# One scan instruction for a whole state, PE's work in whole states, and a diagonal product in every fourth state

## The reference

```python
xs, z = split(h @ in_w);  xs = silu(xs);  proj = xs @ xproj_w     # xs: (L, 512)
dt = softplus(proj[..., :512] + dt_bias)                          # per token and channel
Bm, Cm = proj[..., 512:576], proj[..., 576:]                      # 64 states each
def step(hst, ins):                                               # over the 256 tokens
    hst = hst * exp(dt_t[:, :, None] * A) + (dt_t * x_t)[:, :, None] * B_t[:, None, :]
    y_t = einsum('bds,bs->bd', hst, C_t)
y = ys + xs * Dskip;  return y * silu(z) @ out_w
```

## Time and profile before

| | |
|---|---|
| median of 3 runs (lowest, highest) | 3402.99 us (3399.81, 3408.39) |
| profiled execution, its own time | 3408.53 us |
| its span, first to last instruction | 3406.7 us |
| mean granted TensorE clock | 0.947 |
| PE, ACT, POOL, DVE busy | 3024.2, 2989.0, 2945.7, 2909.5 us |

### The profile page before, as it was taken

One profiled execution on the slowest core, in us unless ns is written; L12 is line 12 of the kernel. 1 busy time (PEld: TensorE's weight loads), 2 busy tenths in 40 slices (PEclk: granted clock), 3 DMA queues, 4 the chain that ended last, 5 costly groups with the idle time before them and its releaser, 6 DMA issues.

```text
span 3406.7 us, 69419 instructions
## 1 busy us (share of the span) xinstructions
PE 3024.2 (89%) x21944; PEld 2683.9 (79%) x21944; DVE 2909.5 (85%) x3331; ACT 2989.0 (88%) x6469; POOL 2945.7 (86%) x1552
## 2 busy tenths in 40 slices
PE   8778898999988999899988999899998899998776
PEld 6568787888878888788877888788887888887765
DVE  3269998899888998889988999889988899899885
ACT  1189999899989999899999999899998999999994
POOL 0069998999888998889988998889988899899995
PEclk6689999999989999899999999899998999999998
DMA  4011111111111111111111111112111111111210
GB/s 174 0 42 43 48 45 47 42 51 48 43 48 47 47 47 42 49 45 48 45 47 43 49 48 43 48 41 52 48 43 46 48 47 46 42 45 45 54 47 26
DMA packets 163033, 162.50 MB, mean 48 GB/s; under 512 B 17610, under 2 KB 156874, under 8 KB 162644
## 3 DMA queue, kind: packets, MB, share of 16 engines
q1 hardware_dynamic: 162644, 157.69, 17.2%
HBM read 154.44 MB, written 3.18 MB: 46 GB/s over the span
## 4 chain that ended last, share of the span: by engine, by line
PE 45%; POOL 16%; ACT 15%; issue 13%; DVE 9%; DMA 1%; DVEq 1%; POOLq 0%; ACTq 0%; SPq 0%
POOL hst L408 12%; PE ps L1225 12%; PE ps L1241 11%; ACT dA L567 7%; PE ps L993 6%; ACT uBT L553 4%; DVE hst L892 4%; PE ps L1002 4%; POOL uBT L417 4%; PE ps L1065 3%; PE ps L1040 2%; PE ps L1114 1%; PE ps L1049 1%; PE ps L1233 1%; PE ps L1150 1%
## 5 line engine op out<-in xcount | busy, mean ns | idle before, releaser
L408 POOL TENSOR_TENSOR hst<-hst,C_sb 128x1024 f32<-128x1024 f32 x1024 | 2441.0, 2409 | 232.8 <-DVE hst L892 226.6
L892 DVE TENSOR_TENSOR_SCAN hst<-dA,ps 128x512 f32<-128x512 f32 x2048 | 2384.0, 1205 | 177.6 <-PE ps L1241 160.1
L567 ACT ACTIVATE dA<-dt,A 128x255 f32<-128x255 f32 x4096 | 1758.5, 504 | 2.8 <-DVE hst L892 2.7
L1225 PE MATMUL ps<-ident,uBT 128*128 128x128 f32 x8192 | 1288.2, 281 | 134.0 <-DVE hst L892 103.0
L1241 PE MATMUL ps<-ident,hst 128*128 128x128 f32 x8192 | 1267.9, 278 | 104.5 <-POOL hst L408 103.7
L1225 PEld LDWEIGHTS ps<-ident,uBT 128*128 128x128 f32 x8192 | 994.2, 145 | 299.0 <-DVE hst L892 152.5
L553 ACT ACTIVATE uBT<-uT,BT 128x512 f32<-128x512 f32 x1536 | 1052.2, 720 | 130.9 <-PE ps L1225 120.0
L1241 PEld LDWEIGHTS ps<-ident,hst 128*128 128x128 f32 x8192 | 979.6, 144 | 139.8 <-POOL hst L408 139.7
L417 POOL TENSOR_TENSOR uBT<-uT,BT 128x512 f32<-128x512 f32 x512 | 559.3, 1092 | 185.3 <-DVE uT L829 185.3
L476 ACT ACTIVATE probs<-ps,nmax 128x128 f32<-128x128 f32 (+1 forms) x256 | 93.9, 423 | 101.6 <-DVE nmax L764 100.7
L993 PE MATMUL ps<-xsT,w_xp 128*128 128x256 f32 x512 | 130.6, 380 | 0.0
(11 more groups left out here) (142 smaller groups left out, 2110.7 us busy)
## 6 DMA issues: line engine op xcount, KB each, us to landing
C_sb<-c_dram SPq DMA_DIRECT2D x1024, 128.0 KB, 2.9
gate_l<-gate_rows_dram SPq DMA_DIRECT2D x16, 256.0 KB, 3.7
x_att<-in_x_dram SPq DMA_DIRECT2D x8, 256.0 KB, 3.0
w<-in_L_cond_W_dram SPq DMA_DIRECT2D x2, 1024.0 KB
out_dram<-x_glu SPq DMA_DIRECT2D x8, 256.0 KB, 3.2
wg<-in_L_cond_mlp_w_dram SPq DMA_DIRECT2D x3, 512.0 KB, 11.4
w_xp<-_L_cond_fwd_xproj_w_dram SPq DMA_DIRECT2D x1, 1280.0 KB, 12.4
w_xp<-_L_cond_bwd_xproj_w_dram SPq DMA_DIRECT2D x1, 1280.0 KB, 15.0
```

Of the source, the lines that this page charges most:

```text
L408: pool.tensor_tensor(h, h, C_sb[:, n % FED:n % FED + 1, :].to_broadcast([P, KI, NB]), ALU.mult).then_inc(hC_ready.sem, 1)
L567: done = act.activation(dA[:, n % NT, c, lo:hi], dt[:, d, c, lo:hi], ACT.Exp, scale=A[:, d, c, n:n + 1])
L892: dve.tensor_tensor_scan(pair(hst[:, n % NR]), pair(dA[:, n % NT]), ps[:, BANK_U + (2 * n + e) % (2 * NU), :][:, way], 0.0, ALU.mult, ALU. ...
L1225: last = pe.transpose(ps[:, BANK_U + (2 * n + e) % (2 * NU), o:o + P], uBT[:, n % NF, j, c * P:(c + 1) * P], ident[:, :])
```

## The change

Four things change.

1. DVE runs one scan instruction of 128x1024 for a state, in the slot e = 1. It waits for whole states: uB_ready, y_mm and scan_done have one event a state.
2. PE works in whole states: sum_state (8 transposes) in slot e = 0, force (8) in slot e = 1. Within a state, sum_state now comes ahead of force.
3. `gate_y` is one state earlier on DVE (ahead of scan 2, before it was between the halves of scan 3).
4. In every fourth state (n % 4 == 3) u is not multiplied by B on ACT and POOL. POOL writes a diagonal, the identity times B, for both halves of tokens (128x2x128 in place of 128x512), and PE computes force as the product of u with this diagonal (8 float32 products in place of 8 transposes). ACT's forcing of this state is gone.

```diff
@@ -43,6 +43,7 @@
     BEHIND = 3
+    by_diagonal = lambda n: n % 4 == 3
     FED = 4
...
@@ -277,8 +278,8 @@
         uT_mm, uT_ready = flow("uT_mm"), flow("uT_ready")
-        uBT_ready, uBT_pooled, uB_ready, dA_ready = flow("uBT_ready"), flow("uBT_pooled", NS // 2), flow("uB_ready", 2), flow("dA_ready", 2)
-        scan_done, hC_ready, y_mm = flow("scan_done", 2, 2 * NT), flow("hC_ready", 1, FED), flow("y_mm", 2, 2 * NR)
+        uBT_ready, uBT_pooled, uB_ready, dA_ready = flow("uBT_ready", NS - NS // 4), flow("uBT_pooled", NS // 2), flow("uB_ready"), flow("dA_ready", 2)
+        scan_done, hC_ready, y_mm = flow("scan_done", 1, NT), flow("hC_ready", 1, FED), flow("y_mm", 1, NR)
         block = ctx.enter_context(nc.Block())
...
@@ -403,7 +404,7 @@
                 pool.wait_ge(C_in[n % FED], (p * (NS // FED) + n // FED + 1) * 16)
-                pool.wait_ge(scan_done.sem, scan_done.at(p * NS + n, 2))
+                pool.wait_ge(scan_done.sem, scan_done.at(p * NS + n, 1))
                 h = hst[:, n % NR]
...
@@ -413,7 +414,11 @@
                 if r_known(p, n) >= NF:
-                    pool.wait_ge(uB_ready.sem, uB_ready.at(p * NS + n, 2 - 2 * NF))
+                    pool.wait_ge(uB_ready.sem, uB_ready.at(p * NS + n, 1 - NF))
+                if by_diagonal(n):
+                    pool.tensor_tensor(uBT[:, n % NF, :, 0:P], ident[:, :].unsqueeze(1).to_broadcast([P, TT, P]),
+                                       BT[:, d, :, n:n + 1].to_broadcast([P, TT, P]), ALU.mult).then_inc(uBT_pooled.sem, 1)
+                    return
                 pool.tensor_tensor(uBT[:, n % NF, 1, :], uT[:, d, DI:2 * DI], BT[:, d, 1, n:n + 1].to_broadcast([P, DI]), ALU.mult).then_inc(uBT_pooled.sem, 1)
...
@@ -543,12 +548,14 @@
             def forcing(p, d, n):
+                if by_diagonal(n):
+                    return
                 r = p * NS + n
...
                 if r_known(p, n) >= NF:
-                    act.wait_ge(uB_ready.sem, uB_ready.at(r, 2 - 2 * NF))
+                    act.wait_ge(uB_ready.sem, uB_ready.at(r, 1 - NF))
                 for j in range(TT - n % 2):
...
@@ -559,8 +566,8 @@
                     act.wait_ge(dt_ready.sem, dt_ready.at(p, 1))
-                if r_known(p, n) >= NT:
-                    act.wait_ge(scan_done.sem, scan_done.at(p * NS + n, (2 if n < NT else e + 1) - 2 * NT))
+                if e == 0 and r_known(p, n) >= NT:
+                    act.wait_ge(scan_done.sem, scan_done.at(p * NS + n, 1 - NT))
                 if n < NT and e == 0:
...
@@ -882,15 +889,18 @@
                 def state(n, e):
+                    if e == 0:
+                        return
                     r = p * NS + n
-                    if n == BEHIND and e == 1 and not very_first:
+                    if n == BEHIND - 1 and not very_first:
                         gate_y(p - 1, 1 - d)
-                    dve.wait_ge(y_mm.sem, y_mm.at(r, e + 1 - 2 * NR))
-                    dve.wait_ge(dA_ready.sem, dA_ready.at(r, e + 1))
-                    dve.wait_ge(uB_ready.sem, uB_ready.at(r, e + 1))
-                    pair = lambda t: t[:, 2 * e:2 * e + 2, :].rearrange("p k n -> p (k n)")[:, way]
-                    dve.tensor_tensor_scan(pair(hst[:, n % NR]), pair(dA[:, n % NT]),
-                                           ps[:, BANK_U + (2 * n + e) % (2 * NU), :][:, way], 0.0, ALU.mult, ALU.add).then_inc(scan_done.sem, 1)
+                    dve.wait_ge(y_mm.sem, y_mm.at(r, 1 - NR))
+                    dve.wait_ge(dA_ready.sem, dA_ready.at(r, 2))
+                    dve.wait_ge(uB_ready.sem, uB_ready.at(r, 1))
+                    bank = BANK_U + 2 * n % (2 * NU)
+                    line = lambda t: t.rearrange("p k n -> p (k n)")[:, way]
+                    dve.tensor_tensor_scan(line(hst[:, n % NR]), line(dA[:, n % NT]), line(ps[:, bank:bank + 2, :]),
+                                           0.0, ALU.mult, ALU.add).then_inc(scan_done.sem, 1)
                 return state
...
@@ -1210,19 +1220,23 @@
                 yield from glu(b)
-            def force(p, n, e):
+            def force(p, d, n):
                 r = p * NS + n
-                if e == 0:
-                    pe.wait_ge(uBT_ready.sem, uBT_ready.at(r, 1))
-                    if n % 2 == 1:
-                        pe.wait_ge(uBT_pooled.sem, uBT_pooled.at(p, n // 2 + 1))
+                if not by_diagonal(n):
+                    pe.wait_ge(uBT_ready.sem, uBT_ready.at(p, n + 1 - n // 4))
+                if n % 2 == 1:
+                    pe.wait_ge(uBT_pooled.sem, uBT_pooled.at(p, n // 2 + 1))
                 if r_known(p, n) >= NU:
-                    pe.wait_ge(scan_done.sem, scan_done.at(r, e + 1 - 2 * NU))
-                for c in range(2 * e, 2 * e + 2):
+                    pe.wait_ge(scan_done.sem, scan_done.at(r, 1 - NU))
+                for c in range(KI):
                     for j in range(TT):
                         o = c % 2 * NB + j * P
-                        last = pe.transpose(ps[:, BANK_U + (2 * n + e) % (2 * NU), o:o + P], uBT[:, n % NF, j, c * P:(c + 1) * P], ident[:, :])
+                        to = ps[:, BANK_U + (2 * n + c // 2) % (2 * NU), o:o + P]
+                        if by_diagonal(n):
+                            last = pe.matmul(to, uT[:, d, j * DI + c * P:j * DI + (c + 1) * P], uBT[:, n % NF, j, 0:P], start=True, stop=True)
+                        else:
+                            last = pe.transpose(to, uBT[:, n % NF, j, c * P:(c + 1) * P], ident[:, :])
                 last.then_inc(uB_ready.sem, 1)
...
@@ -1233,10 +1247,9 @@
                                   start=(c == 0), stop=False, skip_group_check=True)
-            def sum_state(r, n, e):
-                if e == 0:
-                    pe.wait_ge(hC_ready.sem, hC_ready.at(r, 1))
-                for c in range(2 * e, 2 * e + 2):
+            def sum_state(r, n):
+                pe.wait_ge(hC_ready.sem, hC_ready.at(r, 1))
+                for c in range(KI):
                     for j in range(TT):
...
@@ -1245,16 +1258,18 @@
                 def state(n, e):
-                    if n + 1 < NS:
-                        force(p, n + 1, e)
-                    elif not very_last:
-                        force(p + 1, 0, e)
-                    if n == BEHIND and e == 0:
+                    if e == 1:
+                        if n + 1 < NS:
+                            force(p, d, n + 1)
+                        elif not very_last:
+                            force(p + 1, 1 - d, 0)
+                        return
+                    if n == BEHIND:
                         start_y(p, d)
                     if n >= BEHIND:
-                        sum_state(p * NS + n - BEHIND, n - BEHIND, e)
+                        sum_state(p * NS + n - BEHIND, n - BEHIND)
                     elif not very_first:
-                        sum_state(p * NS + n - BEHIND, NS + n - BEHIND, e)
+                        sum_state(p * NS + n - BEHIND, NS + n - BEHIND)
                 return state
```

8 lines of the change are left out of this document (3 added, 5 removed).

## The result

The changed kernel took 3514.26 us (median of 4, 3510.59 to 3517.97), the kernel before 3403.38 us (4 runs beside it). The ratio is 1.0319, 95% interval 1.0303 to 1.0335: 111 us slower. The forecast was 21 us slower, so the sign held and the size did not.

What follows compares the result with a forecast made beforehand. PE was taken to bound some stages, ACT, POOL or DVE others; +4.4 us a pair over 6.5 pairs (+28.6) and -8 in the last pass made +21 us, 3424 us, 0.6% slower, range 3365 to 3475.

Steps and rivals of the forecast that it cites:

- order, whole states, gate_y: Start of a pass: start_y no longer waits for the earlier gate_y, -2.8 us a pair; whole states cost 0.
- products: Every fourth state on PE: 0.905 us more each, +9.1 in PE-full stretches, +0.9 at state 3, +2.0 in heads, a pair.
- relief of ACT and POOL: Every fourth state: less ACT forcing, -3.8 us a pair; POOL's smaller diagonal, -1.0 a pair and -8 in the last pass.
- The step that failed: PE between two scans: force fits by 1.1 us, by 0.2 in every fourth state, so whole states cost 0.
- The 13.2 charged products a pair: Products counted as paid on PE, out of 32 a pair: 10.0 in PE-full stretches, 1 at state 3, 2.2 in heads.
- The second half of the heads: In 1612 to 1662, 4.3 products cost between 0 and 3.9 us a pair; taken as +2.0.
- The last pass: POOL is full and products hide, so 16 smaller diagonals at 0.5 us save 8 us, counted whole, once.
- Passes 0 and 14: Half of the stages each, with losses and gains of 1 to 2 us that were let cancel.
- A (hidden products): PE-full stretches really paced by ACT and DVE, so products are paid half at most: 3385, or 3346 us; chance 0.30.
- B (DVE starves behind the products): In 1527 to 1594 and 1612 to 1662 every fourth scan starts up to 0.9 us late: 3470 us; chance 0.15.
- C (all paid): All 32 products of a pair are paid on PE: +21.4 us a pair, 3534 us; chance 0.02.
- D: Products bring PE's higher clock back sooner, saving up to half of 9.8 us a pair: 3392 us; chance 0.03.

Runs made afterwards that it cites:

- run 1: The changed kernel without diagonals (joined scan, PE in whole states, early gate_y) against the kernel before: 3427.44 us, ratio 1.0061.
- run 3: Diagonals, but 8 transposes of u for the products (B left out there): the changed kernel so cut took 3379.96 us, the same in the old order 3383.55 us.
- runs 2 to 4: Against the kernel before: diagonals alone, 3460.36 us; relief without products, 3379.96 (new order) and 3383.55 us (old); products with the identity, without relief, 3494.40 us.
- Run 6: The changed kernel with 4 products and 4 transposes of u in every fourth state (B left out of half of it): 3453.68 us, ratio 1.0140.
- run 10: The kernel before with diagonals only in passes 0, 14 (but for its state 3) and 15: 3383.43 us, ratio 0.9932.

## Why the prediction was right in sign and wrong in size

The forecast's own terms over the run beside what the experiments measured (us; each difference of two runs is good to some 8; "run 1" is experiment 1, and so on):

| term | forecast | measured |
|---|---|---|
| order, whole states, gate_y | -2.8 x 6.5 = -18 | +23 (run 1) |
| products | (9.1 + 0.9 + 2.0) x 6.5 = +78 | +77 in the old order, +134 in the new (run 3) |
| relief of ACT and POOL | (-3.8 - 1.0) x 6.5 - 8 = -39 | -21 in the old order (-34 beside the products), -47 in the new |
| sum | +21 | 23 + 134 - 47 = +110 |

**The step that failed** is the one on the order: "Waits for whole states leave less play [...] I take 0 and keep the loss as a rival". It was wrong twice. By itself the order costs 23 us, and 41 with the 18 us that I had credited to gate_y: the wait for gate_y fell from 21.0 to 7.7 us in run 1, but PE's wait for scans grew from 103.0 to 154.0, and its whole idle time by 32. And it raised the products' price from 77 to 134 us. Nearly all of that rise is PE's busy time (52 us), with the clock at its lower level for 134 us less in the old order and for only 21 less in the new; why the order takes the clock's gain away stays open, and the forecast had no term for it. The two errors are 41 + 56 = 97 of the miss of 89; relief was 8 better than forecast. In the old order the relief gave less, 21 us: it shortened passes 0, 14 and 15 by some 6 to 7 us each, but a pair in between by 0.2 where 4.8 were forecast. There the lower level took 36.1 us a pair in place of 27.3, and the 2.5 us lost in states 92 to 100 cancel what the other states had gained.

The argument for 0 was that force fits between two scans when these follow each other evenly. It said nothing of the states in which DVE is late with a scan because a chain step stands ahead of it, and there PE's wait is paid in full. It also leaned on DVE's waits for PE where PE is full. The largest piece that the order cost, 2.2 us in states 16 to 24, lies outside these stretches; the next, 1.2 us in 72 to 80, lies inside the heads, where PE, POOL and DVE were all full.

**The products.** Their duration was right (1.78 us). The 13.2 charged products a pair make 86 in the run, and 77 / 0.905 = 85 of 256 would be paid in the old order, in the new 134 / 0.905 = 148. That 86 and 85 meet is luck in part: the 77 us are 159 us more of busy time less 81 of idle time, and the clock, which the count leaves out, had given back up to 67. From start_y to the pass's first product for dt, the stretch that was 38.7 us (1400.81 to 1439.55) is now 41.65 (1446.34 to 1487.99), with three products in it: +2.9, forecast 2.7. The second half of the heads was priced too low. States 72 to 92, which cover the 50 us from 1612 and some more, went from 57.8 to 61.3 us with the diagonals alone, +3.5 where +2.0 was taken and 3.9 was my upper bound; with the order they take 64.0, +6.2. The chain of the kernel after in that stage (start, us, what) shows why:

```profile
1686.21 0.92 PE ps L1254 x8
1687.13 1.79 PE ps L1237 x16
1688.91 0.44 PE ps L1059 x4
1689.35 0.11 PE ps L1071 x2
1689.46 1.06 PE ps L1075 x4
1690.52 1.02 PE ps L1254 x8
...
1700.23 1.79 PE ps L1237 x16
```

There is nothing but PE between the two products, 13.1 us apart: PE did set the pace, and its pipelined ends did not hide idle time.

**Right.** The last pass: -8 forecast, 181.0 to 173.6 us measured (172.9 with diagonals alone). Passes 0 and 14, which I let cancel, were faster by 4.0 and 4.8 us with diagonals alone, a gain that I missed. The diagonal on POOL has a pitch of 0.573 us, near the 0.5 that I took. The joined scan saves nothing: its mean duration fell from 2 x 1205 to 2278 ns, but its pitch is 2 x 1.115 before and 2.20 after, as the DVE timeline of the kernel after shows:

```profile
1704.35 2.28 DVE L902 TENSOR_TENSOR_SCAN hst<-dA,ps 128x1024 f32<-128x1024 f32 x1
1706.55 0.14 DVE L756 RECIPROCAL rsum<-ps 128x2 f32<-128x2 f32 x1
```

**The rivals.** A (hidden products) fell at runs 2 to 4: the relief is real, but the products cost 77 us or more on either order. B (DVE starves behind the products) is right in part: DVE's idle time before its scans rose from 177.6 to 216.7 us, 39 us, where my mark was 40. But 23 of these 39 are there in run 1 without any product (200.5), and with the diagonals alone nothing rose (172.8). In its first stretch, where POOL was full (states 52 to 72), nothing was lost; in its second, the heads, PE itself was the bound. C (all paid) is 20 us from the result, by accident: 148 of 256 were paid, and the order gave the rest. D had the time wrong and the mechanism right: the diagonals alone cut the lower level from 27.3 to 17.0 us a pair and raised the mean granted clock from 0.947 to 0.962. That is up to 5 us a pair, which D forecast, and it lies inside the products' price: without it they would have cost more. The changed kernel has less of it (20.4 us a pair, 0.957). D counted 9.8 us a pair at the lower level, from two stretches; the trace before has 27.3. And the row against D, 7.86 of 11 us busy at full clock, shows that transposes can run at a full clock, not that they hold it as well as products do. The Trainium skill's factor of four for transposes ("TensorE: Matmul & The Clock Gate", Terms) would have put the time at 3570 us, which is nearer to the result than my forecast, and yet isn't its reason: the same eight products still take 1.78 us beside 0.88.

**Open.** The 31 us have no run of their own. By PE's busy and idle time the larger part goes with the clock and the smaller with idle time that is filled less well; why the products bring back less of the clock in the new order is not known. By states, 15 of the 31 lie at the hand-overs; the other 16 have no place yet. Run 6 says that the products' price goes with the load.

## What to carry to other kernels

When the events between two in-order engines become coarser, find out first where in the consumer's order the wait now stands: the same joined instruction cost 23, 164 or 229 us here with three orders of PE's work. Price a change of order on the states in which an engine is late, at hand-overs between chains, not on the even pitch of a full stretch; and don't add the prices of two edits that load the same engine without a run that has both. When the price of PE's work differs between two kernels, split it into busy and idle time and read the granted clock before the difference is put down to waits. Work can be moved to an engine with high load in those passes alone where its trace has room.

## What the runs showed of the hardware

A scan of 1024 elements costs two of 512 within 0.03 us (2.20 and 2.23), since start and end overlap with the neighbours. POOL's diagonal, with 256 elements from two repeated operands, took 0.657 us by its mean duration, and at 0.573 us of pitch it was nearer to half than to all of the 1.00 us for 512. The same 182 PE records took 25.18 us of busy time at a full clock and 28.23 us with 6.8 us at the lower level. With products in place of 2048 of the transposes the time at the lower level fell from 361 to 265 us in the old order and from 350 to 306 in the new; that products as such do this, and not the fuller engine, no run separates. In the old order the whole relief, without a product, is worth 21 us (run 3), and the diagonals of three outer passes, products and all, are worth 21 as well (run 10): in the pairs between, relief of two engines with 86% and 88% of busy time gained 0.2 us, after 8.8 us more at the lower clock.
